# A four-layer network on one core: address reads placed between the products of a routed layer, its ranking moved ahead, and fewer throw-away products in the last stage

## The reference, cut to what matters

```
p = softmax(h @ router.T + router_bias)          # 2048 tokens x 32 experts
chosen = the four largest p of a token; w = p[chosen] / max(sum(p[chosen]), 1e-12)
y[token] = sum over its chosen e of  w[e] * ((silu(h @ gate[e].T) * (h @ up[e].T)) @ down[e].T)
x = x + gb * (y + shared(h))
```

```
for _ in range(SINKHORN_ITERS):                   # 8
    t = t - logsumexp(t, axis=-2, keepdims=True)
    t = t - logsumexp(t, axis=-1, keepdims=True)
gv, idx = jax.lax.top_k(swapaxes(exp(t), -1, -2), m)      # m = 256 / 8 tokens of each expert
out = einsum('bhmei,ehio->bhmeo', routed, experts4) * (gate_values > 0.5)
```

## Time and profile before

| | |
|---|---|
| median of 3 runs | 2133.82 us (2132.87 to 2135.74) |
| profiled execution, its own time | 2131.61 us |
| its span in the profile | 2129.9 us |
| granted clock of PE, mean | 0.864 |
| busy, share of the span | PE 79%, PEld 59%, DVE 70%, ACT 52%, POOL 41% |
| chain that ended last | PE 40%, DVE 21%, ACT 16%, issue 11%, SP queue 5% |
| first half of `l1_ffn`, first shared product to first gather | 1161.3 to 1217.5 us |
| second half, first gather to ACT's last copy | 1217.5 to 1378.6 us |
| `l3_route`, last Sinkhorn product to first expert product | 2070.2 to 2096.0 us |

### The profile page before, as it was taken

The page is one execution under the profiler, slowest core; times in us unless marked ns, Lnnn a source line. Parts: engine busy times, 40 slices in busy tenths (PEclk is TensorE's granted clock), DMA queues, the critical chain, the costliest instruction groups (busy, mean ns, idle before and its releaser), DMA issues.

```text
span 2129.9 us, 40955 instructions
## 1 busy us (share of the span) xinstructions
PE 1673.8 (79%) x13686; PEld 1264.8 (59%) x13686; DVE 1497.1 (70%) x4747; ACT 1117.4 (52%) x3324; POOL 876.3 (41%) x1162
## 2 busy tenths in 40 slices
PE   3788899985287887898789757626777899999979
PEld 3445667773177777787788546512343367777754
DVE  5778766556698898998886732346876577887656
ACT  1444444447888788779733322202453266666620
POOL 3323222033344354343332566465411177777610
PEclk9889999996598798888889978855897899999969
DMA  4111111003000000000001022222101000000000
GB/s 134 47 47 41 33 31 30 17 9 116 15 9 9 17 14 9 11 16 2 2 1 56 27 65 91 96 61 67 53 28 76 14 1 2 2 1 2 1 1 20
DMA packets 67314, 67.72 MB, mean 32 GB/s; under 512 B 9955, under 2 KB 58966, under 8 KB 66566
## 3 DMA queue, kind: packets, MB, share of 16 engines
q1 hardware_dynamic: 58930, 53.09, 7.6%
q0 software_dynamic: 5120, 10.50, 1.8%
q10 hardware_dynamic: 3040, 1.38, 0.2%
HBM read 30.41 MB, written 8.39 MB: 18 GB/s over the span
## 4 chain that ended last, share of the span: by engine, by line
PE 40%; DVE 21%; ACT 16%; issue 11%; SPq 5%; another core or an unknown queue 2%; ACTq 2%; POOL 2%; DMA 1%; DVEq 0%; POOLq 0%
SPq L685 5%; DVE weights L3142 4%; ACT rope_s L4214 3%; ACT rope_c L4214 3%; PE bank L2131 3%; PE bank L1547 3%; PE bank L2091 3%; ACT big L4425 3%; PE bank L1563 3%; PE bank L1740 3%; PE bank L1741 2%; DVE nmax L2699 2%; PE bank L2118 2%; PE bank L2079 2%
## 5 line engine op out<-in xcount | busy, mean ns | idle before, releaser
L2699 DVE TENSOR_REDUCE nmax<-bank 128x4 f32<-128x1024 f32 x144 | 175.9, 1222 | 54.5 <-PE bank L1327 48.7
L887 POOL TENSOR_TENSOR big<-big,rinv 128x512 f32<-128x512 f32 x128 | 131.6, 1048 | 45.7 <-DVE rinv L3746 45.7
L1754 PE MATMUL bank<-V,probsT 128*128 128x9 f32 x1024 | 131.1, 258 | 20.4 <-ACT probsT L4225 20.4
L1754 PEld LDWEIGHTS bank<-V,probsT 128*128 128x128 f32 x1024 | 130.7, 201 | 25.6 <-ACT probsT L4225 23.8
L1740 PE MATMUL bank<-const,big 128*128 128x128 f32 x512 | 120.3, 322 | 12.8 <-DVE hid L3199 9.6
L4029 ACT ACTIVATE feat_o<-bank 128x1024 f32<-128x1024 f32 x72 | 73.7, 1023 | 107.2 <-PE bank L1327 74.2
L4225 ACT ACTIVATE probsT<-bank 128x512 f32<-128x512 f32 x128 | 75.5, 596 | 95.5 <-PE bank L1741 66.6
L4425 ACT ACTIVATE big<-bank,nmax 128x256 f32<-128x256 f32 x256 | 117.6, 477 | 11.1 <-DVE nmax L3740 11.1
L3740 DVE TENSOR_REDUCE nmax<-bank 128x2 f32<-128x512 f32 x128 | 82.0, 683 | 58.1 <-PE bank L2091 58.1
L4029 ACT ACTIVATE O<-bank 128x1024 f32<-128x1024 f32 x72 | 73.7, 1023 | 91.1 <-PE bank L1327 66.9
L1741 PE MATMUL bank<-silu_b,hid 128*128 128x128 f32 x512 | 118.9, 321 | 0.0
(11 more groups left out here) (807 smaller groups left out, 5257.3 us busy)
## 6 DMA issues: line engine op xcount, KB each, us to landing
qT<-parts SPq DMA_DIRECT2D x276, 32.0 KB
big<-V SPq DMA_DIRECT2D x192, 32.0 KB
y_rows<-weights SPq DMA_DIRECT2D x24, 256.0 KB
big<-parts SPq DMA_DIRECT2D x180, 32.0 KB
weights<-in_weights_l_ffn SPq DMA_DIRECT2D x1, 4832.0 KB, 14.3
weights<-in_weights_l_attn SPq DMA_DIRECT2D x1, 3904.0 KB, 13.0
qT<-V SPq DMA_DIRECT2D x96, 32.0 KB
weights<-in_weights_l_ffn SPq DMA_DIRECT2D x1, 2860.0 KB, 11.6
```

What stands on the lines that cost most here:

```text
L887: nc.gpsimd.tensor_tensor(row, row, rinv[:, h % H, :].unsqueeze(2).to_broadcast([P, T, S]), ALU.mult).then_inc(scaled.sem, 1)
L1754: last = mm(pb[1][:, t * S + h * wide:t * S + (h + 1) * wide], probsT[:, h % 2, at:at + P], values_of(b, k)[:, h * wide:(h + 1) * wide], s ...
L2699: V_.tensor_reduce(to, scored.rearrange("p (i a n) -> p i a n", i=HPG, n=n), AX.X, ALU.max, negate=True).then_inc(score_max.sem, 1)
```

## The change

Five edits, in three groups.

1. Ranking. On ACT the exponential stands ahead of the 16 shared steps instead of behind the first. On PE the token turns stand at steps 1 and 3 instead of 4 and 6, the ranking products behind step 5 instead of 8, the naming and the inversion inside step 15, ahead of the last two falls. ACT's copies of the turned tokens move with them. On DVE the weights of the chosen leave `l1_route`, become `l1_weights` and run in the loop, behind the first hidden tiles; since the scores must stay for them, the places of the slots get a buffer of their own.
2. Address reads. `rise_tiles` reads the four addresses of group i + 1, one behind each of its wide products. Only the first group's are read ahead of the loop.
3. `keep_dense` runs 11 and 2 products instead of 20 and 4.

```diff
--- before.py
+++ after.py
@@ -1940,16 +1940,24 @@
                     last = nc.tensor.transpose(pb[0][:, t * P:(t + 1) * P], gathered[i % RING1][:, t, :], C("ident"))
                 last.then_inc(wide_turned.sem, 1)
 
+            def expert_of(tile):
+                return pe.value_load(tile_expert[0:1, tile:tile + 1], min_val=0, max_val=(E1 - 1) * P)
+
             def rise_tiles(i, experts, ph="l1_ffn"):
                 pe.wait_ge(wide_feat.sem, wide_feat(ph, 0, 2 * PAIRS + i + 1))
                 if i >= 2:
                     pe.wait_ge(hid_ready.sem, hid_ready(ph, 0, SHARED1 + i - 1))
                 at = places[ph][0]["gate"][0]
                 both_parts = region[1][:, at:at + 2 * EA * P].rearrange("p (w n) -> p w n", w=2)
+                following = []
                 for t in range(PER_GROUP):
                     last = mm(pb[2 + 2 * (i % 2) + t // 2][:, t % 2 * 2 * P:(t % 2 + 1) * 2 * P].rearrange("p (w n) -> p w n", w=2),
                               gathered_T[i % 2][:, t * P:(t + 1) * P], both_parts[:, :, bass.ds(experts[t], P)], start=True, stop=True)
-                last.then_inc(hid_psum.sem, 1)
+                    if t == PER_GROUP - 1:
+                        last.then_inc(hid_psum.sem, 1)
+                    if i + 1 < GROUPS1:
+                        following.append(expert_of(PER_GROUP * (i + 1) + t))
+                return following
 
             def turn_hidden(i, ph="l1_ffn"):
                 pe.wait_ge(hid_ready.sem, hid_ready(ph, 0, SHARED1 + i + 1))
@@ -1974,22 +1982,22 @@
                         shared_rise(s)
                     if s >= 2:
                         shared_fall(s - 2)
-                    if s in (4, 6):
+                    if s in (1, 3):
                         for u in range(2):
-                            turn_tokens1(s - 4 + u)
-                    if s == 8:
+                            turn_tokens1(s - 1 + u)
+                    if s == 5:
                         rank_tokens()
-                name_tiles()
-                invert_slots()
+                    if s == SHARED1 - 1:
+                        name_tiles()
+                        invert_slots()
                 pe.wait_ge(asked.sem, asked(ph, 0, 9))
                 experts = {}
+                experts[0] = [expert_of(at) for at in range(PER_GROUP)]
                 for n in range(-1, GROUPS1 + 2):
                     if n + 1 < GROUPS1:
-                        experts[n + 1] = [pe.value_load(tile_expert[0:1, at:at + 1], min_val=0, max_val=(E1 - 1) * P)
-                                          for at in range(PER_GROUP * (n + 1), PER_GROUP * (n + 2))]
                         turn_tiles(n + 1)
                     if 0 <= n < GROUPS1:
-                        rise_tiles(n, experts[n])
+                        experts[n + 1] = rise_tiles(n, experts[n])
                     if 0 <= n - 1 < GROUPS1:
                         turn_hidden(n - 1)
                     if 0 <= n - 2:
@@ -2214,7 +2222,7 @@
                 for t in range(T):
                     last = nc.tensor.transpose(pb[1][:, t * P:(t + 1) * P], twice[:, t * P:(t + 1) * P], C("ident"))
                 last.then_inc(sink_sum, 1)
-                keep_dense(pb[7], 20, W("l3_ffn", "experts")[:, 0:4 * D])
+                keep_dense(pb[7], 11, W("l3_ffn", "experts")[:, 0:4 * D])
                 pe.wait_ge(sink_next, SUMS3 + 2)
                 for t in range(T):
                     last = nc.tensor.transpose(pb[0][:, t * P:(t + 1) * P], qT[:, 2, t * P:(t + 1) * P], C("ident"))
@@ -2233,7 +2241,7 @@
                 last.then_inc(rows_psum.sem, 1)
 
             def l3_out():
-                keep_dense(pb[7], 4, W("l3_ffn", "experts")[:, 0:4 * D])
+                keep_dense(pb[7], 2, W("l3_ffn", "experts")[:, 0:4 * D])
                 pe.wait_ge(sink_next, SUMS3 + 3)
                 for u in range(PAIRS):
                     for i in range(2):
@@ -3406,6 +3414,11 @@
                 wide_step_of(V_.tensor_tensor(most, most, tied, ALU.add))
                 wide_settle()
                 V_.tensor_copy(by_expert(chosen_by_expert).rearrange("p e j -> p j e"), most).then_inc(asked.sem, 1)
+
+            def l1_weights():
+
+                of_expert = lambda v: v.rearrange("p (j e) -> p j e", e=E1)
+                score, most = of_expert(rows(8, 2)), of_expert(rows(12, 2))
                 wide_step_of(V_.tensor_tensor(score, score, most, ALU.mult))
                 wide_settle()
                 wide_step_of(V_.tensor_reduce(one, score, AX.X, ALU.add))
@@ -3415,12 +3428,13 @@
                 wide_step_of(V_.reciprocal(total, one))
                 wide_settle()
                 wide_step_of(V_.tensor_tensor(weights_all, score, spread(total, E1), ALU.mult))
+                wide_settle()
 
             def l1_slots(ph="l1_ffn"):
 
                 of_expert = lambda v: v.rearrange("p (j e) -> p j e", e=E1)
                 per_expert = lambda v, n: v.unsqueeze(2).to_broadcast([P, E1, n])
-                most, place = of_expert(rows(12, 2)), of_expert(rows(8, 2))
+                most, place = of_expert(rows(12, 2)), of_expert(rows(26, 2))
                 upto, before, over = rows(20, 2), rows(24, 2), by_expert(rows(22, 2))
                 before_e, count_e = by_expert(before), by_expert(upto)[:, :, N16 - 1]
                 dve.wait_ge(ranks_psum.sem, ranks_psum(ph, 0, 1))
@@ -3501,7 +3515,7 @@
             def l1_pick_weights(k):
 
                 of_expert = lambda v: v.rearrange("p (j e) -> p j e", e=E1)
-                place, same = of_expert(rows(8, 2)), of_expert(rows(20, 2))
+                place, same = of_expert(rows(26, 2)), of_expert(rows(20, 2))
                 wide_step_of(V_.tensor_tensor(same, place, slots_of[:, :, k:k + 1].to_broadcast([P, N16, E1]), ALU.is_equal))
                 wide_settle()
                 wide_step_of(V_.tensor_tensor(same, same, weights_all, ALU.mult))
@@ -3548,6 +3562,8 @@
                         hidden_tiles(n)
                     if n:
                         take_hidden(n - 1)
+                    if n == 0:
+                        l1_weights()
                     if n == 1:
                         l1_rows()
                     if 2 <= n < 2 + TOP1:
@@ -4355,6 +4371,8 @@
 
             def l1_ffn(ph="l1_ffn"):
                 wide_front(ph)
+                act.wait_ge(asked.sem, asked(ph, 0, 1))
+                nc.scalar.activation(rows(10, 2), rows(8, 2), ACT.Exp).then_inc(answered.sem, 1)
                 for s in range(SHARED1):
                     act.wait_ge(hid_psum.sem, hid_psum(ph, 0, s + 1))
                     if s >= 2:
@@ -4362,14 +4380,11 @@
                     two = 2 + 2 * (s % 2)
                     nc.scalar.activation(shared_silu[s % 2], pb[two][:], ACT.Silu)
                     nc.scalar.activation(up_copy[s % 2], pb[two + 1][:], ACT.Copy).then_inc(silu_g.sem, 1)
-                    if s == 0:
-                        act.wait_ge(asked.sem, asked(ph, 0, 1))
-                        nc.scalar.activation(rows(10, 2), rows(8, 2), ACT.Exp).then_inc(answered.sem, 1)
                     if s in (6, 10, 14):
                         take_shared(s // 4 - 1)
-                    if s in (5, 7):
+                    if s in (2, 4):
                         for u in range(2):
-                            take_tokens1(s - 5 + u)
+                            take_tokens1(s - 2 + u)
                 take_shared(PAIRS - 1)
                 for n in range(-1, GROUPS1 + 2):
                     if n + 1 < GROUPS1:
```

## The result

The changed kernel took 2120.62 us (median of four runs, 2117.02 to 2122.09) against 2133.62 us of the kernel before: ratio 0.9944, interval 0.9927 to 0.9960. It is 13.0 us faster where 28.9 us were forecast. The profiled execution took 2117.02 us (span 2115.3), 3.6 us under its median. 3.4 of these lie ahead of everything that was changed (the first shared rise starts at 1157.89 us for 1161.31), so places are compared by their distance from that rise.

The account below looks back on a forecast made before the run. It took the loop to be bound by waits, VectorE to bind ahead of it and PE at the end. 2131.6 - 5.5 - 20 - 3.4 = 2102.7, 2104.9 on the runs' scale; predicted 2105, range 2094 to 2124.

Parts of the forecast that it names:

- Start, 5.5 us: Ahead of the loop: ranking sooner brings the first gather 5.5 us sooner, range 3 to 7.
- my second way to the number: Start: PE's step 15 ends at 1206.0, then names and four inversion quarters to 1210.3 against 1215.98, 5.7 us sooner.
- Weights in the loop: Loop: DVE's weights behind the first hidden tiles slow up to four gathers by 0.26 us each, 1 us.
- Reads, 20 us: Loop: address reads between wide products remove PE's pause and clock fall; 141 us for 161.1, 20 us gained, best 27.7.
- the 15 of my sum: Behind the last gather: 1.6 us of landing, 11.8 us from last turn to ACT's end, 1.6 us of arrears.
- The signals keep the loop at its pace: Loop: waits for PE without reads keep the pair at 11.75 us; loop gives 0 to 6 us, 2124; chance 0.22.
- A read that stands alone is dearer: Loop: separate address reads cost more, a group takes 5.3 us, loop gives 13 us, 2112; chance 0.12.
- Every read stops the array: Loop: PE's array waits at each read, up to 7.0 us a group, loop loses 26 us, 2151; chance 0.06.
- End, 3.4 us: Last phase: fewer throw-away products gain 4.9 us less 1.5 for a clock fall, 3.4 us, range 1.5 to 5.
- Signs to look for: Profile after: first gather near 1212, no 2.4 us pauses, gathers 1.25 us apart, loop 138 to 144 us, clock above 0.95.
- the first rival: Loop: late PE signals, not reads, set the pace; pairs of 11.7 us would prove it; 2124, chance 0.22.

Follow-up runs that it names:

- the first comparison: All five edits together against the kernel before, chip not known: 2120.62 us against 2133.62, ratio 0.9944.
- the first run without reads: Changed kernel with the loop's address reads replaced by constant experts (tile t takes expert t/3), on chip 1: 2085.6 us, 0.9956 against the kernel before.

## Why the forecast was wrong, step by step

- **Start, 5.5 us: right** (5.6). The exponential came 2.4 us sooner for 2.6, the scan 8.5 for 8. The slots lost 2.9 us beside POOL where I had taken 1.5 from bounds of 0 and 4; the last quarter waits 1.14 us for VectorE, not for PE as in my second way to the number.
- **Weights in the loop: right, and smaller.** One gather took 1.44 us instead of 0.94 beside them, 0.5 us for the 1 us taken. By the Trainium skill's rule (SBUF — State Buffer, "SBUF: two separate sides") it could have been up to 2.6, the length of the five operations in the trace after; the trace shows 0.5. On chip 1 it was 0.1 us.
- **Reads, 20 us: wrong.** They gave 2.6 us alone where signals are late (from a loss of 1.3 to a gain of 6.2), 6.4 beside the other parts, and cost 4.4 on chip 1. The sentence that failed is "POOL becomes the bound, even if PE's signals stay as late as they are". I added the 2.43 us of pause and the 1.3 us of clock to what a pair costs, as if the pair were the sum of PE's times. The earlier trace rows spoke against it: the pair at the granted clock of 1.00 had 1.3 us less of busy PE than the other and took 11.80 us for 11.75. In a loop whose pace comes from elsewhere both are slack: when the pause went, PE stood as long one step later, for ACT's copy, which stood 5.97 us for PE's own late signal. The signals' rhythm (eight gathers at 1.25 us and a stop of 1.75 make 11.75) was in the earlier trace rows and in the 17.9 us that POOL stood. I had read those 17.9 us as a remainder, of which 6 would stay. Had I divided them by the count of stops, I should have seen one stop of about 1.75 us for every second group, which no read on PE explains. After the change POOL stands the same 17.9 us, and behind the last gather lie 20.6 us instead of the 15 of my sum; these two terms make the 158.5 us with the 120 of the gathers. Where signals are prompt the step fails as well: POOL binds, but it did so before.
- **Rivals.** "The signals keep the loop at its pace" (2124) was the right one; it took 1 us for the loop where 2.6 came. "A read that stands alone is dearer" describes chip 1 and does not decide there: reads start some 0.78 us apart between the products and 0.64 in a row, and PE is busy 0.7 us more a group. By my estimate from the Trainium skill (DMA: Bandwidth & Descriptors, "Latency and other measured facts") a group would have taken 5.3 us; seen are 5.0 on chip 1 and 5.87 elsewhere. "Every read stops the array" did not come: where signals are prompt the reads make the loop 2 us longer, and with late signals 161.4 us for 161.1 alone.
- **End, 3.4 us: right way, too small** by 1.4 (4.8 in the trace; 1.9 and 3.2 as times on chip 1, where the range of 1.5 to 5 holds both). I took off 1.5 us for one fall of the clock. PE did stand 2.81 us and ran its next four passes at 0.76 us each instead of 0.45, at the lower of its levels at first, but VectorE's winner was ready at 2080.19 and they ended at 2080.25, so next to nothing of the slow passes lay on the path: the gain is the 4.7 to 5.2 us that I had before that subtraction.
- **Signs to look for.** The first gather (near 1212, was 1208.5, and 1211.9 with the shift of 3.4) and the vanished 2.4-us pauses came true. PE's idle time at the end was 2.8 us for 3. Gathers "nearly throughout" 1.25 apart, a loop of 138 to 144 us and a clock above 0.95 did not. Two signs came in part: the last quarter of the inversion still waits 1.14 us for VectorE, and VectorE's wait at the end is 0.78 us, not under 0.5. The pairs of 11.7 us, named as the proof of the first rival, came.

## What to carry to other kernels

An idle stretch of an engine in a steady loop is worth something only if the loop's period is made of it; find first which wait repeats with the period, and what ends it. A wait whose releaser has no name while the producer's work is long done is a term of its own: hold the producer's end against the waiter's start, and look at what every other engine did at that instant. And run the kernel before on more than one chip before a mechanism is believed: the first run without reads would have "shown" the wrong cause. Where a record of signals is used, count first how many of them it has.

## What the runs showed of the hardware

- While POOL issues indirect gathers one behind another, on chips 3, 7 and 8 and in the first comparison PE's semaphore signals are posted up to about 5 us behind the product in the steady loop, most of them together, about 1.7 us after POOL's last gather. Plain DMAs of the same size from SyncE do not do it on chip 3, nor do half the bytes change it on chip 7.
- It takes a run of gathers: in the changed kernel's first trace and in the kernel that waits behind every four (`landing`) no recorded signal was late whose product ended within 3.8 us of POOL's restart.
- On chip 1 no signal of PE in this loop is late, and the kernel before is 38 us (1.8%) faster, 28 of them in this loop and 7 beside the gathers that bring the rows of y back (133.3 us for 140.1). Beside those gathers PE's signals are late on chip 1 too, up to 1.5 us (up to 4.3 in the trace before). What makes the chips differ was not found.
- Every recorded signal of ACT and VectorE in the loops came within 0.01 us. But where PE's are late, records are missing: in the trace before 18 of 58 signals of ACT, 20 of 54 of VectorE, 18 of 79 of PE, and two thirds of the landings of POOL's gathers (843 of 2560 are there). On chip 1 (fewer throw-away products alone) none of the engines' signals is missing and 2482 of 2560 landings are there, with plain DMAs on chip 3 all 1536. So more than PE's signals may be concerned; whether the delay is in them or in what carries them was not found.
- Reads of addresses between the products lengthen the array's busy time, though the sequencer does them: 62.34 us busy for 52.80 in the same 70 us at the same granted clock of 1.00 (2.4 GHz).
